# Self-attention scored twice, the second time transposed with the maximum inside the matmul

## What is computed

```
q, k, v = (layernorm(x) @ sign(W).T) * (mean|W| * scale)     # 32 q heads, 8 k/v heads, 32 wide
scores  = einsum('bhqd,bhkd->bhqk', q, k) / sqrt(32)
attn    = softmax(scores, axis=-1)
out     = einsum('bhqk,bhkd->bhqd', attn, v)
x       = x + (out @ sign(Wo).T) * (mean|Wo| * scale_o)
```

## Time and profile before

| | us |
|---|---|
| median of 3 runs | 1619.93 |
| lowest, highest | 1618.73, 1621.06 |
| the profiled execution | 1617.47 |
| its span | 1615.7 |

### The profile page before, as it was taken

One profiled execution on the slowest core, in us unless ns is written; L12 is line 12 of the kernel. 1 busy time (PEld: TensorE's weight loads), 2 busy tenths in 40 slices (PEclk: granted clock), 3 DMA queues, 4 the chain that ended last, 5 costly groups with the idle time before them and its releaser, 6 DMA issues.

```text
span 1615.7 us, 24334 instructions
## 1 busy us (share of the span) xinstructions
PE 1442.4 (89%) x8774; PEld 1090.0 (67%) x8774; DVE 972.0 (60%) x1700; ACT 843.7 (52%) x2416; POOL 352.8 (22%) x341
## 2 busy tenths in 40 slices
PE   5898799979998899886898989887899999999998
PEld 3566566656665666665676757665688888888886
DVE  4588636773677357744765748466374574573545
ACT  5598306761577147702674747565354444454442
POOL 3011200130013001221211212103243242242331
PEclk9999799999999999997999999999899999999999
DMA  4444133233323242225553735434710130220111
GB/s 171 117 128 120 54 103 84 63 105 88 89 61 103 75 112 63 79 92 158 161 167 89 189 99 154 115 88 127 281 55 0 43 115 1 78 78 1 65 66 53
DMA packets 98603, 157.15 MB, mean 97 GB/s; under 512 B 14646, under 2 KB 52788, under 8 KB 98484
## 3 DMA queue, kind: packets, MB, share of 16 engines
q1 hardware_dynamic: 98484, 155.60, 32.7%
HBM read 82.15 MB, written 25.17 MB: 66 GB/s over the span
## 4 chain that ended last, share of the span: by engine, by line
PE 67%; ACT 9%; DVE 9%; issue 5%; SPq 4%; DMA 3%; POOL 2%; ACTq 0%; DVEq 0%; POOLq 0%
PE bank L872 14%; PE bank L884 7%; PE bank L799 7%; PE bank L744 6%; PE bank L700 4%; ACT prob L952 4%; PE bank L717 4%; PE bank L758 3%; PE bank L654 3%; PE bank L857 3%; PE bank L776 3%; PE bank L812 3%; PE bank L733 2%; PE bank L897 2%; SPq L1490 2%
## 5 line engine op out<-in xcount | busy, mean ns | idle before, releaser
L952 ACT ACTIVATE prob<-bank,neg_max 128x256 f32<-128x256 f32 x768 | 356.7, 488 | 34.5 <-DVE neg_max L1166 34.5
L1166 DVE TENSOR_REDUCE neg_max<-bank 128x2 f32<-128x512 f32 x384 | 260.6, 683 | 103.4 <-PE bank L717 64.5
L744 PE MATMUL bank<-ident,prob 128*128 128x128 f32 x1536 | 231.7, 274 | 2.1 <-DVE probT L1174 1.6
L744 PEld LDWEIGHTS bank<-ident,prob 128*128 128x128 f32 x1536 | 177.1, 141 | 9.3 <-issue 4.3
L1425 POOL TENSOR_TENSOR v_lo<-v_all,v_hi 128x512 fp32r<-128x512 f32 x88 | 122.7, 1396 | 247.4 <-ACT v_hi L1026 247.4
L717 PE MATMUL bank<-k_stack,q_stack 128*128 128x256 f32 x512 | 132.2, 342 | 44.3 <-ACT prob L952 42.4
L952 ACT ACTIVATION_READ_ACCUMULATOR prob<-bank,neg_max 128x1 f32 x768 | 170.1, 221 | 0.0
L961 ACT ACTIVATE probT<-bank 128x512 f32<-128x512 f32 x160 | 96.0, 600 | 139.6 <-PE bank L744 136.0
L1174 DVE COPY probT<-bank 128x512 f32<-128x512 f32 x224 | 152.2, 680 | 4.2 <-PE bank L744 4.2
L717 PEld LDWEIGHTS bank<-k_stack,q_stack 128*128 128x128 f32 x512 | 82.6, 189 | 106.8 <-ACT prob L952 73.7
L872 PE MATMUL bank<-pT_hi,v_hi 128*128 128x512 f32 x352 | 137.4, 390 | 2.6 <-POOL v_lo L1425 2.6
(11 more groups left out here) (159 smaller groups left out, 2862.2 us busy)
## 6 DMA issues: line engine op xcount, KB each, us to landing
q_stack<-hi_lo SPq DMA_DIRECT2D x384, 64.0 KB, 2.0
xin<-x_scratch SPq DMA_DIRECT2D x33, 512.0 KB, 4.5
xq_stack<-xhi_lo SPq DMA_DIRECT2D x128, 128.0 KB, 2.4
x_res<-in_x SPq DMA_DIRECT2D x19, 512.0 KB, 3.8
x_scratch<-x_res SPq DMA_DIRECT2D x16, 512.0 KB, 2.9
xin<-in_ctx SPq DMA_DIRECT2D x16, 512.0 KB, 4.8
x_group<-x_scratch SPq DMA_DIRECT2D x32, 256.0 KB, 3.7
x_scratch<-x_group SPq DMA_DIRECT2D x32, 256.0 KB, 2.6
```

The costliest lines, as they stand in the source:

```text
L744: t = pe.transpose(T[:, kt * SEQ + qt * P:kt * SEQ + (qt + 1) * P], Pb[:, qt * SEQ + kt * P:qt * SEQ + (kt + 1) * P], ident[:, :])
L952: t = act.activation(Pb[:, a * SEQ:(a + 1) * SEQ], S[:, a * SEQ:(a + 1) * SEQ], ACT.Exp, bias=mx[:, a:a + 1], accum_out=total)
L1166: dve.tensor_reduce(neg_max[n % 4][:, 0:QT], scores[n % 3][:, :].rearrange("p (a b) -> p a b", a=QT), AX.X, ALU.max, negate=True).then_inc ...
```

## The change

Self-attention is scored twice.
- "pre" (head by head, as "score" before, over 96 rows instead of 128) is there for the row maxima only: VectorE writes them negated to neg_top. It runs LEAD = UH + 3 = 11 heads ahead.
- "top", once a unit: TensorE transposes the 128 x 16 maxima, ScalarE copies them as a hi row part, VectorE makes the lo part, and SyncE puts both with two DMAs into rows 96 and 97 of q_stack, whose ring has three buffers now. k_stack holds ones in these two rows ("ones").
- "tile": k as weights, two heads' q as 512 moving columns, 98 rows: the bank holds score minus maximum, transposed, keys on the partitions. ScalarE takes the exponential of 512 columns in one instruction, without a sum, to a ring of eight PT tiles. No flip and no evacuation follow.
- "mix" is the old "values", reading PT. GpSimd adds pairs of tiles ("fold"); "sums" multiplies the folds with ones, so that each head's sum stands on 32 rows. "finish": ScalarE copies the mixed bank; VectorE turns the sums in 32 x 32 blocks, takes reciprocals of one column in 32, turns them back and multiplies.
- The normed result is split in fp16 hi and lo, and signs_o is fp16. For the range, v's row scale is divided by its largest value, which is multiplied to o's.
- The q chunks stand at other slots, the work between groups is in another order, and slots are written out in `self_order` itself. Cross-attention keeps its steps; only its counts start at zero now.

The core of the diff:

```diff
+LEAD = UH + 3
+PT_RING, FOLD_RING = 8, 4
@@ self_order
-    order += value(0, 0) + value(0, 1) + whole_q(0, 1) + key(0, 1)
+    score = lambda g, i: ("pre", g * GROUP_HEADS + i)
+    top = lambda U: [("top", U), ("top_out", U)]
+    meet = lambda g: [p for c in range(KB) for p in (("q", g, 1, c), score(g, c))] + [("q_out", g, 1)]
+    order += [("row_v", 0), ("row_v_out", 0)] + value(0, 0) + value(0, 1)
+    order += meet(0) + flip_sign(3) + key(0, 1) + top(0) + [score(0, i) for i in range(UH, LEAD)]
...
-            put(0, 1, *proj(g - 1, 7))
-        for u in range(KV_HEADS - 2):
-            for i in range(KB):
-                at = max(0, u * UH + 6 - KB + i)
-                chunk = [("q", g, u + 2, i)] + ([("q_out", g, u + 2)] if i == KB - 1 else [])
-                put(0, at, *chunk)
+            put(0, 0, *proj(g - 1, 6))
+            put(0, 2, *proj(g - 1, 7))
+        for tq in range(2, KB):
+            for c in range(KB):
+                chunk = [("q", g, tq, c)] + ([("q_out", g, tq)] if c == KB - 1 else [])
+                put(0, max(0, (tq - 2) * UH - 6 + c), *chunk)
...
+        for i in range(GROUP_HEADS + 8):
+            step = []
+            if i < GROUP_HEADS:
+                step.append(("tile", g * GROUP_HEADS + i))
+            if i + LEAD < GROUP_HEADS:
+                step.append(score(g, i + LEAD))
+            step += side.get(i, [])
+            if i >= 5 and (i - 5) % 4 == 0 and i - 5 < GROUP_HEADS:
+                step.append(("mix", (g * GROUP_HEADS + i - 5) // 4))
+            if i >= 6 and (i - 6) % 4 == 0 and i - 6 < GROUP_HEADS:
+                s = (g * GROUP_HEADS + i - 6) // 4
+                step += [("sums", s)] + ([("finish", s // GB)] if s % GB else [])
+            if i % UH == 5 and i // UH + 1 < KV_HEADS:
+                step += top(g * KV_HEADS + i // UH + 1)
...
+            order += [("norm", "x", n, 2)] + turn("x", n, 0) + late[0] + [("load", "x", n, 3)]
+            order += turn("x", n, 1) + late[1] + turn("x", n, 2) + [("norm", "x", n, 3)] + turn("x", n, 3)
+            order += key(n, 0) + whole_q(n, 0) + proj(g, 0) + value(n, 0) + proj(g, 1) + [("o_load", g, 2)]
+            order += value(n, 1) + proj(g, 2) + meet(n) + proj(g, 3) + [("o_load", g, 3)] + key(n, 1) + top(n * KV_HEADS)
+            order += proj(g, 4) + [score(n, i) for i in range(UH, LEAD)] + proj(g, 5)
@@ tensor_program
+            elif kind == "pre":
...
                 for step in (("q_out", g, tq), ("k_out", g, tq // (P // HD))):
                     s = STACK[step]
                     e.wait_ge(stacked[s % 2], 192 * (s // 2 + 1))
+                if n > 1:
+                    e.wait_ge(sem["pre_maxed"], n - 1)
                 for a in range(QT):
+                    t = pe.matmul(tops[n % 2][:, a * SEQ:(a + 1) * SEQ],
+                                  qst[U % 3][0:SUB, r, b * SEQ + a * P:b * SEQ + (a + 1) * P],
+                                  kst[0:SUB, tq, b * SEQ:(b + 1) * SEQ], start=True, stop=True)
...
+            elif kind == "top":
+                e.wait_ge(sem["pre_maxed"], (U + 1) * UH)
+                pe.transpose(J[0:REP * GB * QT, 0:P], neg_top[U % 2][:, :, :, :].rearrange("p r b a -> p (r b a)"),
+                             ident[:, :]).then_inc(full, 1)
+            elif kind == "tile":
...
+                e.wait_ge(top_stacked[U % 2], 32 * (U // 2 + 1))
+                if m > 1:
+                    e.wait_ge(sem["tile_exped"], m - 1)
+                pe.matmul(tiles[m % 2][:, :], kst[0:SUB + 2, tq, b * SEQ + kt * P:b * SEQ + (kt + 1) * P],
+                          qst[U % 3][0:SUB + 2, 2 * hp:2 * hp + 2, b * SEQ:(b + 1) * SEQ],
+                          start=True, stop=True).then_inc(sem["tiled"], 1)
...
+            elif kind == "sums":
+                for r in range(REP):
+                    t = pe.matmul(summed[r * HD:(r + 1) * HD, b * SEQ:(b + 1) * SEQ], ones[:, 0:HD],
+                                  fold[(2 * s + r // 2) % FOLD_RING][:, r % 2 * SEQ:(r % 2 + 1) * SEQ],
+                                  start=True, stop=True, tile_position=(0, r * HD))
@@ scalar_program
+            elif kind == "tile":
+                act.activation(PT[m % PT_RING][:, :], tiles[m % 2][:, :], ACT.Exp).then_inc(sem["tile_exped"], 1)
@@ vector_program, "finish"
+                dve.transpose(sum_cols[:, :], summed[:, :]).then_inc(sem["sum_turned"], 1)
...
+                dve.tensor_tensor(OTn[:, :], OTs_self[:, :], R_sb[:, :], ALU.mult).then_inc(sem["attn_out"], 1)
@@ gpsimd_program
+            if kind == "tile" and at[0] % 2:
...
+                pool.tensor_tensor(fold[f % FOLD_RING][:, :], PT[2 * f % PT_RING][:, :], PT[(2 * f + 1) % PT_RING][:, :],
+                                   ALU.add).then_inc(sem["folded"], 1)
@@ sync_program
-                            sp.dma_start(qst[U % 2][a * HD:(a + 1) * HD, i, :].bitcast(F32),
+                            sp.dma_start(qst[U % 3][a * HD:(a + 1) * HD, i, :].bitcast(F32),
                                          b[i * HD:(i + 1) * HD, part, :].bitcast(F32)).then_inc(stacked[s % 2], 16)
+            elif kind == "top_out":
...
+                for part in range(2):
+                    e.wait_ge(sem["top_lo" if part else "top_hi"], U + 1)
+                    sp.dma_start(qst[U % 3][SUB + part:SUB + part + 1, :, :].bitcast(F32),
+                                 top_rows[U % 2][:, part, :].bitcast(F32)).then_inc(top_stacked[U % 2], 16)
```

More of the change, by code:

```diff
@@ L46, with attention_order @@
 AHEAD = 3
+LEAD = UH + 3
+GROUP_HEADS = KV_HEADS * UH
 SELF_UNITS = NG * KV_HEADS
 SELF_HEADS = SELF_UNITS * UH
-SELF_SETS = SELF_HEADS // REP
-ON_SCALAR_SELF, ON_SCALAR_CROSS = (1, 4, 6), (1, 3, 5, 7)
+ON_SCALAR = (1, 3, 5, 7)
+PT_RING, FOLD_RING = 8, 4
 QB, VB, OB = KB, KB + KT, KB + 2 * KT
 NSC = OB + KB
-def attention_order(first, heads, per_unit, per_set, side, lead, end, copy, fin):
+def attention_order(first, heads, side, lead):
     order = []
@@ L82, in attention_order @@
             m = n - 1
-            if m % per_set == per_set - 1:
-                order.append(("values", (first + m) // REP if first < SELF_HEADS
-                              else SELF_SETS + (first + m - SELF_HEADS) // 2))
-            if m % per_unit == per_unit - 1:
-                unit = ((first + m) // UH if first < SELF_HEADS
-                        else SELF_UNITS + (first + m - SELF_HEADS) // XUH)
-                order.append((end, unit))
-                finish += [[(copy, unit)] if copy else [], [(fin, unit), (fin + "_out", unit)]]
+            if m % 2 == 1:
+                order.append(("values", (first + m) // 2))
+            if m % XUH == XUH - 1:
+                unit = (first + m) // XUH
+                order.append(("xend", unit))
+                finish += [[("xcopy", unit)], [("xfin", unit), ("xfin_out", unit)]]
     late = rest
@@ L108, in self_order @@
         norms = [0, 1] if j == 0 else [j + 1] if j + 1 < TILES else []
-        items.append(([("norm", "x", 0, m) for m in norms], turn("x", 0, j, 0) + turn("x", 0, j, 1)))
+        items.append(([("norm", "x", 0, m) for m in norms], turn("x", 0, j)))
     for i in first[TILES:]:
@@ L163, in self_order @@
             put(last, 6, ("norm", "x", g + 1, 1))
-        lead = [proj(g - 1, 6)] if g else []
-        body, late = attention_order(g * KV_HEADS * UH, KV_HEADS * UH, UH, REP, side, lead, "end", None, "fin")
-        order += body
+        late = []
+        for i in range(GROUP_HEADS + 8):
[12 more added lines that the diff above has]
+                step += top(g * KV_HEADS + i // UH + 1)
+            if i < GROUP_HEADS:
+                order += step
+            elif step:
+                late.append(step)
@@ L178, in self_order @@
+            order += value(n, 1) + proj(g, 2) + meet(n) + proj(g, 3) + [("o_load", g, 3)] + key(n, 1) + top(n * KV_HEADS)
+            order += proj(g, 4) + [score(n, i) for i in range(UH, LEAD)] + proj(g, 5)
+        else:
+            for step in late:
+                order += step
             for i in range(2 * TILES):
@@ L780, in tensor_program @@
                 t.then_inc(sem["valued"], 1)
-            elif kind == "fin":
-                U = at[0]
-                J, full, use = bank_of("fin_out", U)
-                e.wait_ge(sem["recip_all"], U + 1)
-                bank_free(e, "fin_out", U)
-                for a in range(4):
-                    t = pe.transpose(J[:, a * P:(a + 1) * P], r_all[:, a, :, :].rearrange("p r d -> p (r d)"),
-                                     ident[:, :])
-                t.then_inc(full, 1)
             elif kind == "o":
```

360 lines of the change are left out of this document (199 added, 161 removed).

## The result

The changed kernel takes 1811.23 us (median of 4 runs, 1809.99 to 1816.04); the kernel before took 1620.49 beside it (1618.73 to 1624.15). The ratio is 1.1179, interval [1.1151, 1.1207]: 191 us slower, where the prediction said 161. The profiled execution of after has a span of 1808.2 us at a mean granted clock of 0.909 (before 0.98). Cross-attention and feed-forward take 925 us in both; everything lies in self-attention, whose bodies end at 883 instead of 690.

The account below looks back on a forecast made before the run. Serial q and top transfers through SyncE bound TensorE: 18.05 us a unit, 19.7 with the low clock. Self-attention ends at 853.5 instead of 690, 163 later, less 2 for the output projection: 1781 us, range 1710 to 1845.

Parts of the forecast that it names:

- q full to pre 9.85: Self-attention, each unit: from q projection's end to its first pre, twelve SyncE issues and landing, 9.85 us.
- The unit: Self-attention bodies: one unit of 8 heads takes 19.7 us, against 13.35 in the kernel before.
- The clock: TensorE behind each q wait: low clock makes pre, chunk, mix and top 3.9 us instead of 2.2.
- Rival 1: The order's distance doesn't bind, q lands within 4.8 us of q full: unit 11.5, whole 1557 us; chance 0.08.
- Rival 4: Transfers partly hidden, by faster SyncE issues or top rows landing in 1 us: 1660 to 1715 us; chance 0.06.
- Rival 3: TensorE's clock never falls in self-attention: 18.05 us a unit, whole 1740 us; chance 0.2.
- Rival 2: TensorE stays at the low clock through the self-attention bodies: 23.5 us a unit, whole 1857 us; chance 0.08.
- two top transfers and 16 slots without q: End of each group's body, behind the last waited pre's unit: remaining transfers and slots take 22.3 us.
- Wrong: Refuting signs: pre under 6 us behind q_out, or first waits on folds or maxima, about 1 us a unit each.
- no engine above 65% in the bodies: Sign expected in the self-attention bodies: every engine busy at most 65% of the time.
- The output projection in fp16: Output projection falls from 3.72 to 3.46 us each, 8 us over 32, of which 2 lie at the end.
- Between groups: From one group's body to the next: 67 us, 72 behind group 0, with 13 until the keys start.

Follow-up runs that it names:

- e4: The changed kernel with 22 matmuls that nobody reads before each pre that waits for a new q; 1789.11 us, ratio 1.1056.
- e6: The changed kernel with q chunks four slots earlier and a q_stack ring of four buffers instead of three; 1882.71 us, ratio 1.1623.
- e8: The changed kernel with ring of four, q chunks four slots earlier, second key tile in slot 6, GpSimd's hi and lo one slot later; 1856.32 us.
- e3: The changed kernel with q chunks four slots earlier and the ring still of three buffers; 1914.36 us, ratio 1.1837.

## Why the prediction was right, and where it was off

The side, the mechanism and the place were right; the time was 30 us short, within the range. That it wasn't further off is in part luck: one term was 48 us too small, and the others together 18 too large. By its steps, the working being in the prediction:

| term | predicted | measured |
|---|---|---|
| first tile of group 0 | 83 | 80.8 |
| from there to the first waited pre, group 0 / others | 15.0 / 20.8 | 16.4 / 19.5 |
| a unit (five in a group) | 19.7 | 19.9, 19.0, 19.0, 18.8 |
| last waited pre to the body's end | 26.3, then 22.3 | 41.7, 36.1, 32.8, 30.4 |
| between groups | 72, 67, 67 | 66.9, 68.1, 67.3 |
| bodies end | 853.5 | 883 |

- *q full to pre 9.85*: 9.7 in the chain above. Twelve issues of 0.59 and a landing of 1.98 carry over unchanged from the earlier trace rows; 384 of them again, median 590 ns.
- *The unit*: right within 1 us in all groups, and its pieces too. The sum of the twenty came out 10 us lower. Where the top rows land in 1.84, the path from their copy to the tile is 2.75 (353.12 to 355.87 with filled waits), not 3.7; with the late landings it is 3.45 in the mean of the twenty, which is 5 of the 10.
- *The clock*: 1.65 a unit predicted, as 3.9 instead of 2.2 (rounded). The 3.9 is what after shows; at full clock e4 shows 1.93, so 2.0 is the price in that slot. It was right also that the low level ends in slots 6 and 7 within the series (1.00 from 350 on).
- *Rival 1* (the distance doesn't bind) is out: the waits stand at the pre line. *Rival 4* is out with the unit of 19.2, issues of 0.59 and a top landing of 1.8 at the least. *Rival 3* is out by the clock rows.
- *Rival 2* (the clock stays low) came half true, at the ends of the groups only: 0.50 over the 14 us from 442 to 456.
- *The step that failed* is "two top transfers and 16 slots without q: 3.1 + 3.7 + 6 + 4 + 5.5 = 22.3". It measured 30 to 36, and 41.7 in group 0: 48 us too small over four groups (15.4 + 13.8 + 10.5 + 8.1), of which the other terms took back 18. That leaves the 30. The slots without q were priced at full clock, and they don't get it: over the four stretches, 141 us, TensorE is busy for 115 at granted clocks of 0.71, 0.64, 0.66 and 0.84 in the mean, and at 0.50 a value set takes 1.87, not 1.00 (the earlier trace rows had that row). An estimate from these figures, busy time times clock, gives some 81 us of work at full clock, so 34 of the 48. The other part is the folds behind the finish on GpSimd, named under "Wrong" with 1 us a unit, hidden behind the q wait. At the ends no q wait hides them, and all of TensorE's 11.8 us for folds stand there, 2.4 to 4.2 a group. But they weigh less than their wait: from e6 to e8, which moves settle (and the keys), the wait falls from 15.0 to 1.6 and the four stretches from 140.5 to 137.1 only. Why the clock stays low at the ends is open. With filled waits (e4) it fell at a group's end all the same (0.50 from 422 to 438), so there it is not the q wait that brings it down.
- *A sign that was wrong*: "no engine above 65% in the bodies". TensorE is busy 73 to 76% of them (113.92 of 150.90 us in group 1), since work at the low clock fills time.
- *The output projection in fp16*: 3.72 to 3.46 predicted; 3.45 to 3.47 in the chain.
- *Between groups*: right within 5 us, for the stated reason; before the last turn TensorE waits for the norm (the row L670 <- xin, 26.6 us; 13 us to the key's start predicted, 13.2 measured), and the rest is SyncE's issues.

The chain of after at a group's start, for that last point; the load L1533 behind the store, the other eleven issues of L1554 and the two of L1575 are left out:

```profile
292.08 2.89 DMA x_scratch<-x_res
...
302.26 0.59 SPq L1554
...
305.40 0.50 PE bank L750
```

A load that waits for a store, twelve issues for the keys, then the top rows: no engine's computing is in that chain for 13 us. It is D's pattern, and the prediction had it in this place, but not as a rule for the rest; that is why e3 and e6 were expected 200 us too low.

## What to carry to other kernels

Where one queue issues all transfers in order, place each by when it is needed and by what it is ahead of: moving twelve issues one slot, from ahead of two urgent ones to behind them, was worth 182 us of 1880. A change that takes work off TensorE, VectorE and ScalarE can lose a tenth of the time when it halves the distance between a producer and its consumer; compare that distance, in slots times us a slot, with the path in the trace first. And price the ends of a loop with rows taken at the clock that TensorE gets there: the same slots took 30 to 42 us where 22 to 26 had been reckoned at full clock.

## What the hardware showed unexpectedly

- A DMA of 64 KB between two SBUF buffers into 32 partitions lands 2.0 us after its issue, one of 256 KB 5.6 (4.1 to 9.5), at the same 0.6 us of issue. From the first issue to the last landing twelve of the one kind take 8.9 us for 768 KB, three of the other 7.9.
- The top rows' DMAs, 8 KB each, land in 1.8 us at the median, hardly less than 64 KB. Seven of the 32 pairs take up to 3.9, and these are the seven beside which a 16 KB packet of instructions is loaded; one of the pair's 32 completions then comes 1.2 to 2.0 us behind the others.
- The clock stayed at 0.50 for 14 us in which TensorE was busy for 12.76, behind four us with 2.10 busy and no single wait over 1.4. In part of that stretch the loads of the next group moved 318 GB/s (440 to 448); whether that has to do with it wasn't tried.
- VectorE's multiply of 128 x 512 (two inputs in SBUF) and GpSimd's fold hold each other up, and the one that starts second pays. In after no fold overlaps it and all 32 take 0.69 us. With a lead of ten a fold is already running in 27 of 32, and these take 1.11 to 1.41 (1.12 at 282.31), each ending 0.55 us behind the fold. With the finish in three slots the multiply often starts first: it takes 0.67 (300.53), and the fold that starts 0.18 behind it 1.62 instead of 1.27.
